# Ternary quantisation shared between VectorE and GpSimd, and three groupings of neighbouring work changed, in a post-norm layer of linear attention and a ternary FFN on eight cores

## The reference

```
# attention: 16 heads, 4 kv heads, D = 128
sq, sk = elu(q) + 1, elu(k) + 1
kv   = einsum('bhsd,bhse->bhde', sk, v)
qkv  = einsum('bhsd,bhde->bhse', sq, kv)
norm = einsum('bhsd,bhd->bhs', sq, sk.sum(axis=2))
attn = (qkv / (norm[..., None] + 1e-6)) @ Wo.T
# FFN: w1 is 8192 x 2048, w2 is 2048 x 8192
scale = mean(abs(w)); wq = sign(w) * (abs(w) >= 0.7 * scale)
h = gelu(x1 @ w1q.T + b1);  out = h @ w2q.T + b2
```

## Time and profile before

| | us |
|---|---|
| timed runs of the kernel | 5131.21 and 5246.88, median 5189.04 |
| the profiled execution, its time | 5129.48 |
| the profiled execution, its span on the slowest core (core 7) | 5127.9 |
| spans of the other cores | 5078.1 to 5113.5 |
| mean granted TensorE clock, cores 0 to 7 | 0.794 to 0.801 |

### The profile page before, as it was taken

How to read it: one execution, slowest core, us unless ns; L and a number is a source line. 1 busy time by engine, 2 the same in 40 slices (tenths; PEclk the granted TensorE clock), 3 DMA queues, 4 the chain that set the end, 5 groups by cost and what they waited for, 6 DMA issues and landing times.

```text
span 5127.9 us, 42520 instructions; the slowest of 8 cores (5078.1 to 5127.9 us)
## 1 busy us (share of the span) xinstructions
PE 2946.2 (57%) x11722; PEld 1193.0 (23%) x11722; DVE 1756.7 (34%) x3187; ACT 1045.0 (20%) x1473; POOL 493.9 (10%) x774
## 2 busy tenths in 40 slices
PE   2444445549765535555344342199960999609996
PEld 0111112113222112222111110033420444204442
DVE  0122223336433367777666664200123001230013
ACT  1566665553200100000000000011000110001100
POOL 1000000000011113333222221000000000000000
PEclk8677667769889768888666666599985999859998
DMA  9545554331233337777444442144521444214442
GB/s 168 160 148 152 154 156 108 107 103 29 56 103 95 105 86 185 184 184 191 133 135 142 147 130 77 64 136 152 150 88 58 137 151 155 88 61 138 150 156 107
DMA packets 215232, 644.62 MB, mean 126 GB/s; under 512 B 30674, under 2 KB 34770, under 8 KB 202708
## 3 DMA queue, kind: packets, MB, share of 16 engines
q1 hardware_dynamic: 161716, 486.66, 32.0%
q0 software_dynamic: 53280, 155.24, 10.8%
HBM read 578.87 MB, written 100.66 MB: 133 GB/s over the span
## 4 chain that ended last, share of the span: by engine, by line
PE 33%; DMA 26%; DVE 23%; ACT 8%; issue 8%; DVEq 1%; POOL 1%; ACTq 0%; SPq 0%; POOLq 0%
PE PB L825 16%; PE PB L770 11%; DMA arnE<-w 9%; DVE arnC L697 6%; DMA arnE<-xt 5%; DVE arnE L689 4%; DVE arnE L694 4%; PE PB L448 4%; DMA arnC<-w1q 3%; ACT arnE L263 3%; ACT arnE L268 3%; DMA out<-arnB 3%; DMA arnB<-y1s 2%; DMA w1q<-arnC 1%; PE PB L392 1%
## 5 line engine op out<-in xcount | busy, mean ns | idle before, releaser
L770 PE MATMUL PB<-arnB,arnC 128*128 128x512 bf16 x4096 | 984.7, 399 | 813.3 <-DMA arnC<-w1q 509.9
L825 PE MATMUL PB<-arnA,arnC 128*128 128x512 bf16 x4096 | 957.2, 399 | 432.4 <-DVE arnC L697 432.4
L770 PEld LDWEIGHTS PB<-arnB,arnC 128*128 128x128 bf16 x4096 | 403.2, 102 | 1399.0 <-issue 1008.6
L825 PEld LDWEIGHTS PB<-arnA,arnC 128*128 128x128 bf16 x4096 | 414.6, 102 | 974.6 <-issue 537.8
L838 DVE TENSOR_TENSOR arnB<-arnE,arnB 128x512 f32<-128x512 f32 x64 | 44.3, 692 | 1460.3 <-ACT arnE L834 1460.3
L779 ACT ACTIVATE arnA<-PB,b_sb 128x512 bf16<-128x512 f32 x256 | 176.4, 689 | 1076.8 <-PE PB L770 1076.8
L697 DVE SCALAR_TENSOR_TENSOR arnC<-arnE 128x512 bf16<-128x512 f32 x512 | 354.5, 692 | 95.6 <-DVE arnE L694 25.3
L564 PE MATMUL PB<-arnB,arnC 128*128 128x512 bf16 x1024 | 266.9, 422 | 149.0 <-DVE arnE L581 147.1
L263 ACT ACTIVATE arnE<-arnE 128x1024 f32<-128x1024 f32 x256 | 270.7, 1057 | 229.1 <-DMA arnE<-w 170.6
L834 ACT ACTIVATE arnE<-PB,b_sb 128x512 f32<-128x512 f32 x64 | 44.1, 689 | 1246.6 <-PE PB L825 1246.6
L275 DVE SCALAR_TENSOR_TENSOR acc<-acc_t,acc 128x1 f32<-128x1 f32 x256 | 40.8, 159 | 695.1 <-ACT arnE L268 691.4
(11 more groups left out here) (144 smaller groups left out, 1875.2 us busy)
## 6 DMA issues: line engine op xcount, KB each, us to landing
arnE<-w SPq DMA_DIRECT2D x256, 512.0 KB, 3.6
arnE<-w SPq DMA_DIRECT2D x512, 256.0 KB, 3.6
arnC<-w1q SPq DMA_DIRECT2D x192, 512.0 KB, 3.3
arnC<-w2q SPq DMA_DIRECT2D x96, 1024.0 KB, 5.9
w1q<-arnC POOLq DMA_DIRECT2D x256, 128.0 KB, 4.8
w2q<-arnC POOLq DMA_DIRECT2D x256, 128.0 KB, 2.7
arnE<-xt POOLq DMA_DIRECT2D x64, 256.0 KB, 3.9
y1s<-arnE POOLq DMA_DIRECT2D x64, 256.0 KB, 2.4
```

Of the source, the lines that this page charges most:

```text
L770: e.matmul(o, l, r, start=s, stop=z),
L825: e.matmul(o, l, r, start=s, stop=z),
```

## The change

Four things are done:

- In quant_piece the first compare (tb) and the difference (tqv, now tensor_tensor in place of scalar_tensor_tensor) go to GpSimd. The second compare (tg) stays on VectorE and waits for the load and for the tqv of the piece before. The lists vlast and clast, which held the tokens of the last pieces, go.
- emit_qkv and emit_qkv_B become one function again: the broadcast matmul is issued in the same step as the two read-out matmuls, and follows them in TensorE's queue. The read-out uses PB2 and PB3 alone. The waits for attnT_tok[15] at the start of the output projection go, since its banks PB5 and PB6 are used by nothing else by then.
- emit_ln1_dc is written into the loop over tiles: the first layer norm of tile t runs at the start of tile t, for all t, behind the whole last loop of the tile before.
- The bias of an output block is added on VectorE (tensor_scalar) and no longer on ScalarE (L834).

Core of the diff:

```diff
-    def emit_qkv_B():
-        ic, t, qp, j, tqkv, tr = qkv_pend.pop(0)
-        tbc = p.op("tensor", ... PB[4] <- ones_k1, row(2 + j) ...)
+    def emit_qkv(ic, t):
+        tqkv = p.op("tensor", ... PB[2] <- kv_l, sq_t ...
+                    waits=[sq_toks[ic][t], t_kv_ev, qkv_free], inc=sT)
+        tnrm = p.op("tensor", ... PB[3] <- ks_l, sq_t ...
+                    waits=[nrm_free], inc=sT)
+        tu = p.op("scalar", ... Ln ...);  tr = p.op("scalar", ... Exp ...)
+        tbc = p.op("tensor", lambda e, o=PB[4].ap(), l=ones_k1.ap(), r=r_r:
                    e.matmul(o, l, r, start=True, stop=True),
                    waits=[tr, rbc_free], inc=sT)
...
             sq_toks[ic][t] = m4_
-            emit_qkv_B()
             if ic >= 1:
                 emit_qkv(ic - 1, t)
...
-        tb = p.op("vector", lambda e, o=Esl(9), a=stage, b2=tneg:
+        tb = p.op("gpsimd", lambda e, o=Esl(9), a=stage, b2=tneg:
                   e.tensor_scalar(o, a, -C1H, b2, ALU.subtract, ALU.is_le),
-                  waits=[tok_d, thr_done, qres["b_free"],
-                         sqprev if first else None,
-                         abs_guard if first else None], inc=sV)
+                  waits=[tok_d, thr_done, qres["b_free"][0],
+                         abs_guard if first else None], inc=sP)
         tg = p.op("vector", lambda e, o=Esl(2), a=stage, b2=tpos:
                   e.tensor_scalar(o, a, C1H, b2, ALU.subtract, ALU.is_ge),
-                  inc=sV)
-        tqv = p.op("vector", lambda e, o=dst, a=Esl(2), b2=Esl(9):
-                   e.scalar_tensor_tensor(o, a, 1.0, b2, ALU.mult,
-                                          ALU.subtract),
-                   waits=[tb, tg] + list(dst_waits), inc=sV)
+                  waits=[tok_d, thr_done, qres["b_free"][1],
+                         sqprev if first else None], inc=sV)
+        tqv = p.op("gpsimd", lambda e, o=dst, a=Esl(2), b2=Esl(9):
+                   e.tensor_tensor(o, a, b2, ALU.subtract),
+                   waits=[tb, tg] + list(dst_waits), inc=sP)
         qres["stage_free"][sl] = tqv
-        qres["b_free"] = tqv
+        qres["b_free"][0] = tqv
+        qres["b_free"][1] = tqv
         tw = dma("gpsimd", dram_dst, dst, waits=[tqv])
...
     for t in range(NT):
-        for dc in (range(DC) if t == 0 else []):
-            emit_ln1_dc(t, dc)
+        for dc in range(DC):
+            (the body of emit_ln1_dc, with Esl(0) in place of Esl(1))
...
-            tv1 = p.op("scalar", lambda e, o=Esl(0), a=PB[2 + par].ap(),
+            tv1 = p.op("vector", lambda e, o=Esl(0), a=PB[2 + par].ap(),
                        b=b2_sb.ap()[:, dc:dc + 1]:
-                       e.activation(o, a, AF.Identity, bias=b),
-                       waits=[tmm, t_b2, ytmp_free], inc=sC)
+                       e.tensor_scalar(o, a, b, None, ALU.add),
+                       waits=[tmm, t_b2], inc=sV)
...
             x1_ready[dc] = None
-            if t + 1 < NT:
-                emit_ln1_dc(t + 1, dc)
```

More of the change, by code:

```diff
@@ L381, in build_nc @@
     thr_done = None
-    qkv_pend = []
-    def emit_qkv_B():
-        nonlocal rbc_free
-        if not qkv_pend:
-            return
-        ic, t, qp, j, tqkv, tr = qkv_pend.pop(0)
-        tbc = p.op("tensor", lambda e, o=PB[4].ap(), l=ones_k1.ap(),
-                   r=row(2 + j):
+    def emit_qkv(ic, t):
+        nonlocal qkv_free, nrm_free, rbc_free
+        kvh = ic // 4
+        kv_l = kvsb.ap()[:, kvh * 129: kvh * 129 + 128]
+        ks_l = kvsb.ap()[:, kvh * 129 + 128: kvh * 129 + 129]
+        sq_t = sq_tile(ic, t)
+        tqkv = p.op("tensor", lambda e, o=PB[2].ap(), l=kv_l, r=sq_t:
+                    e.matmul(o, l, r, start=True, stop=True),
+                    waits=[sq_toks[ic][t], t_kv_ev, qkv_free], inc=sT)
+        tnrm = p.op("tensor", lambda e, o=PB[3].ap()[0:1, :], l=ks_l, r=sq_t:
+                    e.matmul(o, l, r, start=True, stop=True),
+                    waits=[nrm_free], inc=sT)
+        qkv_last_mm[ic] = tnrm
+        j = (ic * NT + t) % 2
+        u_r, r_r = row(0 + j), row(2 + j)
+        tu = p.op("scalar", lambda e, o=u_r, a=PB[3].ap()[0:1, :],
+                  b=c_eps_at.ap():
+                  e.activation(o, a, AF.Ln, bias=b),
+                  waits=[tnrm, uro[j], st_["c_eps_at"],
+                         t_bkr if ic == 0 else None,
+                         t_bvr if ic == 0 else None], inc=sC)
+        nrm_free = tu
+        tr = p.op("scalar", lambda e, o=r_r, a=u_r, s2=c_none.ap():
+                  e.activation(o, a, AF.Exp, scale=s2),
+                  waits=[st_["c_none"]], inc=sC)
+        tbc = p.op("tensor", lambda e, o=PB[4].ap(), l=ones_k1.ap(), r=r_r:
                    e.matmul(o, l, r, start=True, stop=True),
@@ L400, in emit_qkv_B @@
                    o=Bbf[:, ic * 2048 + t * 512: ic * 2048 + (t + 1) * 512],
-                   a=PB[2 if qp == 0 else 5].ap(), b=Esl(0):
+                   a=PB[2].ap(), b=Esl(0):
                    e.tensor_mul(o, a, b), waits=[tqkv], inc=sV)
-        qkv_free[qp] = tdv
+        qkv_free = tdv
         if t == NT - 1:
             attnT_tok[ic] = tdv
[L407 to L436, removed]
     for ic in range(16):
@@ L664, in build_nc @@
     out_last = None
-    qres = {"rr": 0, "stage_free": [None] * 4, "b_free": None,
+    qres = {"rr": 0, "stage_free": [None] * 4, "b_free": [None, None],
             "wr_w1": [[None] * 4 for _ in range(64)],
-            "wr_w2": [[None] * 16 for _ in range(16)], "lastB": None,
-            "lastV": None, "usedC": False, "usedV": False}
+            "wr_w2": [[None] * 16 for _ in range(16)], "lastB": None}
     gwr_w1 = [[], []]
@@ L711, in w2q_slot @@
         return Cap[:, 4096 + (i % 3) * 4096: 4096 + ((i % 3) + 1) * 4096]
[L713 to L733, removed]
-    for t in range(NT):
-        for dc in (range(DC) if t == 0 else []):
-            emit_ln1_dc(t, dc)
+    for t in range(NT):
+        for dc in range(DC):
+            x1d = Bfap[:, dc * 512:(dc + 1) * 512]
+            x1b = Bbf[:, 16384 + dc * 512: 16384 + (dc + 1) * 512]
+            tld = dma("sync", x1d, y1s[t, dc],
+                      waits=[y1_wr[t][dc], x1_free[dc],
+                             wo_mm_done if t == 0 else None])
+            ta1 = p.op("vector", lambda e, o=Esl(0), a=x1d, b=Abc1(t):
+                       e.tensor_mul(o, a, b),
+                       waits=[tld, ab_done[t],
+                              y_free[0] if (t == 0 and dc == 0) else None,
+                              y_free[1] if (t == 0 and dc == 0) else None],
+                       inc=sV)
+            ta2 = p.op("vector", lambda e, o=x1d, a=Esl(0), b=Bbc1(t):
+                       e.tensor_add(o, a, b), inc=sV)
+            x1_ready[dc] = ta2
+            x1bf_ready[dc] = p.op("vector", lambda e, o=x1b, a=x1d:
+                                  e.tensor_copy(o, a), inc=sV)
         for fc in range(NFC):
@@ L751, in build_nc @@
                     wtoks.append(tw)
-                    if cf:
-                        clast = tqv
-                    else:
-                        vlast = tqv
-                w1q_tok[par] = [x for x in (vlast, clast) if x is not None]
+                w1q_tok[par] = tqv
                 gwr_w1[par] = wtoks
             else:
-                w1q_tok[par] = [dma(
+                w1q_tok[par] = dma(
                     "sync", buf, w1q[fc],
-                    waits=[w1q_free[par]] + qres["wr_w1"][fc] + gwr_w1[par])]
+                    waits=[w1q_free[par]] + qres["wr_w1"][fc] + gwr_w1[par])
                 gwr_w1[par] = []
```

42 lines of the change are left out of this document (12 added, 30 removed).

## The result

The changed kernel is slower: the ratio of its time to that of the kernel before is 1.2555, with a 95% interval of 1.2481 to 1.2629. Its fastest run took 6411 us, the fastest of before beside it 5111 us. The forecast was 5640 us with a range of 5380 to 6050; the sign was right, but the growth forecast, 510 us, is two fifths of the 1285 us that came, and the time lies outside the range. The profiled execution took 6414.5 us (span 6412.9, core 7, mean granted clock 0.738), against 5129.5 us (0.801). Times are compared between executions in which both dies ran at the same clock; durations of single instructions are in some cases (b_pool, c_fill, b_spw3 and the three kernels that take the compare apart) read from an execution in which one die was slower.

A forecast was written before the change was run, and what follows sets the result against it. No single engine bounds the kernel; each stage has its own limit, tile 0 running at the pace of VectorE's quantised pieces. 5129.5 + 620 (pieces) + 185 (read-out) - 295 (seams) = 5640 us, range 5380 to 6050.

The forecast's parts named there:

- pieces: 512 P - 1070: Tile 0's weight quantisation: growth from 512 pieces of period P on GpSimd; +620 us at P = 3.3.
- read-out in one step: Q stage: broadcast matmul waits for ScalarE's Exp, a group takes 8.26 instead of 5.24 us; +185 us.
- three seams: Between token tiles: separating the layer norm from the output loop saves 98.4 us at each seam; -295 us.
- bias on VectorE: Tile 0's w2 half: eviction takes about 0.75 us instead of 0.69 in the same chain; no growth counted.
- P = 1.34 + tb + tqv: Period of one quantised piece on GpSimd: DMA issue and its delay, two gaps, compare and difference in series.
- I take 3.3, a little under the middle: Chosen piece period in us, between 2.02 and 4.87, leaving 1.96 us for GpSimd's two passes, 1.7 times VectorE's.
- The upper end of P, 4.87: Longest piece period in us: each GpSimd pass as long as VectorE's 2048-column memset, 1.77 us.
- The prediction's estimate from that page: Piece period from the Trainium skill's GpSimd figures: P about 3.2, a sum some 50 us under the forecast.
- 13.5: Tile 0's w2 half: us per output block beyond its pieces, VectorE waiting for TensorE and eviction, then adding; unchanged.
- rival (c): Q stage: stalls lower TensorE's clock; if all 60 groups were slow, +270 us, 5910 us; chance 4%.
- (a): Tile 0's pieces: GpSimd as quick as VectorE, 4984 us at P = 2.02; chance 3% faster, 5% within 2%.
- (b): Tile 0's pieces: VectorE's and GpSimd's compares exclude each other, P = 4.0, 5998 us, up to 6443; chance 15%.

The follow-up runs named there:

- b_pool: The kernel before with only the first compare and the difference of each piece moved to GpSimd; ratio 1.2600.
- c_fill: The kernel before with the one-step attention read-out plus 13 unused matmuls per group while TensorE would wait; ratio 1.0304, fastest 5264 us.
- b_spw3: Compare and difference on GpSimd, each write DMA issued by SP four pieces later, otherwise the kernel before; fastest 6073 us.
- the three kernels that take the compare apart: Kernel before, compare and difference on GpSimd, the compare cut to one operation, made an addition, or given a constant operand; only durations read.
- g_bias: The kernel before with only the bias of an output block added by VectorE instead of ScalarE; ratio 1.0016.
- a_seams: The kernel before with only the next tile's first layer norm moved out of the last loop, behind it; ratio 0.9397, fastest 4799 us.
- b_spw: Compare and difference on GpSimd, each write DMA issued by SP ahead of the next piece's load, otherwise the kernel before; ratio 1.576.

## Why the prediction was wrong in size, by its own steps

| step | predicted us | in the changed kernel's trace us |
|---|---|---|
| pieces: 512 P - 1070 | +620 (P = 3.3) | +1289 (1239 + 1336 - 1286) |
| read-out in one step | +185 | +265 (830 - 565) |
| three seams | -295 | -296 |
| bias on VectorE | 0 | 0 (g_bias: ratio 1.0016) |
| sum on 5129.5 | 5640 | 6388, measured 6414.5 |

**The step that failed is a choice of value.** The sum's frame, P = 1.34 + tb + tqv, held: with 2.00 and 1.26 it gives 4.60, and 4.71 was measured; the rest is a DMA issue of 0.60 instead of 0.54, and gaps of 0.21 and 0.04 where I had 0.10 and 0.10. What failed was "I take 3.3, a little under the middle", with 1.96 us for both passes. They took 3.26, so the term for the pieces, +620 us, should have been +1289. The upper end of P, 4.87, held the truth, but I gave the upper part only 7% and cut the range there. That it held was in part luck: it let no pass take longer than 1.77 us, the compare took 2.00, and the sum stayed below it only because the difference took 1.26. The reason I gave, that these passes have 512 columns and the upper row 2048, was an argument about size, while the unknown was the engine. A common factor on VectorE's rows misled too: VectorE's tensor_scalar has 486 ns for two operations, less than its two-input pass of 692, and on GpSimd the order is reversed, 2001 against 1261. The factors are 4.1 and 1.8, and a common one of 1.7 fitted only the second. The Trainium skill (GPSIMD Engine Reference, section 3.1) has 769 ns for a one-input loop of 512 elements at its best; the measured 2001 ns, and 1567 with one operation, decide against it as a price for tensor_scalar. Its ratio of about two for two-input passes is near the 1.8 here, where VectorE's instruction was a scalar_tensor_tensor. The prediction's estimate from that page was, unrounded, P = 3.23 and 36 us under its sum and not some 50.

In the w1 half the stretch gives 4.84 us a piece (1239/256), and from the first L675 (2139.94) to the 256th (3357.71) it is 4.78. For the w2 half, TensorE's blocks:

```profile
3570.28 9.36 PE L784 MATMUL PB<-arnA,arnC 128*128 128x512 bf16 x32 [39.01 <-POOL arnC L675]
...
3656.28 4.00 PE L784 MATMUL PB<-arnA,arnC 128*128 128x512 bf16 x9 [39.01 <-POOL arnC L675]
```

86.0 us a block (3570.28 to 3656.28), where 16 x 4.71 + 13.5 would be 88.9. The next block's first compare runs on GpSimd from 3609.10, while VectorE still waits for TensorE, and only the difference waits for VectorE:

```profile
3621.44 1.26 POOL L675 TENSOR_TENSOR arnC<-arnE 128x512 bf16<-128x512 f32 x1 [10.34 <-DVE arnE L671]
```

So a block adds 10.6 us to its pieces (86.0 - 16 x 4.71) and not 13.5, and the formula was good to 3 us in 86.

**The read-out** was right in mechanism, and short by the clock. One line of ScalarE and three of TensorE in the changed kernel:

```profile
1443.05 0.72 ACT L404 ACTIVATE rows<-rows,c_none 1x512 f32<-1x512 f32 x1
...
1443.91 1.09 PE L407 MATMUL PB<-rows,ones_k 1*128 1x512 f32 x2 [2.91 <-ACT rows L404]
...
1444.94 5.31 PE L432 MATMUL PB<-arnA,arnC 128*128 128x512 bf16 x16
...
1453.69 1.09 PE L407 MATMUL PB<-rows,ones_k 1*128 1x512 f32 x2 [2.91 <-ACT rows L404]
```

L404 ends at 1443.77 and L407 starts 0.14 us later; it occupies 1.03 us. From the start of L432 to that of the next L407 it is 8.75 us, so the group takes 9.78 where I had 8.26. Of the 31 groups behind the last weights pass (1271.75 to 1582.91) 20 take 9.78 us, 9 about 11.1 and 2 take 8.09, as in c_fill; these two have the same pause of 2.9 us ahead of matmuls at the full clock. On average a group grew by 4.75 us there, and by 3.6 in the first eight blocks, where part of the wait hides beside the weights pass. The prediction's rival (c) had all groups wholly cold, +270 us on top of the sum, with a chance of 4%. What came is +80 on top, because most groups were partly cold (at the lower clock): 5.31 us lies between the 3.6 of warm and the 7.1 of cold matmuls. I had read that the w1 half of tile 0 with a mean clock of 0.86 has pauses of this kind, and charged 4 us for it and all else beyond the 181. This is the second term that was too small, by 80 us. c_fill settles that it is the pause.

**The seams** were right. The first output multiply and the last cast of the first seam, and TensorE there:

```profile
4754.00 0.69 DVE L857 TENSOR_TENSOR arnE<-arnB,arnE 128x512 f32<-128x512 f32 x1
...
4812.90 0.43 DVE L707 CAST arnB<-arnB 128x512 bf16<-128x512 f32 x1
```

```profile
4789.72 2.29 PE L736 MATMUL PB<-arnB,arnC 128*128 128x512 bf16 x5 [36.69 <-DMA arnC<-w1q]
```

4754.00 to 4813.33 is 59.3 us against 59.7 predicted and 158.1 before; the -296 in the table is three times this difference, and a_seams took 298 us off by itself. The DMA rate did not hold it.

**The rivals.** (a) is out by far. (b), that both engines shut each other out, is not what happened in the changed kernel: VectorE's compare fits, but for 0.06 us, in the 0.60 us before GpSimd's issue, and GpSimd's compare has 2000 to 2056 ns in all 512 cases. Its time of 5998 us came nearer than mine, by another cause, and that is luck. Where the two compares do start together (b_spw, b_spw3), GpSimd's grows by 0.27 us and VectorE's 0.49 stays; where GpSimd's starts first, VectorE's grows by 0.1 to 0.4 us. The Trainium skill (SBUF: State Buffer, section Who interferes with whom) has the second one blocked for the whole instruction of the first, if VectorE is in a 2-port mode (no run here shows in which mode it was); the runs agree that the second one waits, but VectorE's wait behind GpSimd's 2.00 us is 0.4 us at most.

## What to carry to other kernels

Before work is moved to an engine that does no arithmetic in the trace, its price per pass is the first thing to measure, and a range must keep the whole unknown: here the trim cut off what came, and even the untrimmed bound held for the sum of the two passes only, not for the compare. An engine that runs one piece's chain including its DMA issues pays for each link in series, so count the issue too (1.2 of 4.7 us), and do not put a waiting write in front of a load that ought to run ahead (b_spw: 1.58 against 1.26). Interleaving two loops is not an overlap when each step waits for a DMA round trip in order; separating them saved 6% here. A TensorE pause of 2.9 us in each group cost more than its length here (4.54 us in a group of 9.78), because the matmuls after it were slower. The largest gain on the kernel before that was found, 9%, needs none of the moves to another engine: it comes from the seams and from not letting VectorE's queue stand behind TensorE.

## What the runs showed of the hardware

- GpSimd on 128 x 512 float32: tensor_scalar with two operations 2.00 us, with one 1.57, with two operations whose operands are both constants 1.93; tensor_tensor with bf16 output 1.26. VectorE: 0.486 and 0.69.
- A GpSimd DMA issue starts 0.60 us after the instruction it waits for ends, both where VectorE's instruction released it and where GpSimd's own did, and takes 0.54 to 0.71 us.
- A tensor_scalar of each engine at the same time: started together, GpSimd's 2.00 becomes 2.27 and VectorE's stays at 0.49 (b_spw, b_spw3); VectorE's started 0.07 us behind takes 0.89, some 0.36 us behind 0.60, and GpSimd's stays at 2.00 (b_spw).
- 16 matmuls of 512 columns after a pause of 2.9 us mostly took 5.3 us instead of 3.6: the first nine or so are 0.43 us apart and the rest 0.21. In two groups of 31 they took 3.6 after the same pause. 13 unused matmuls in the pause made the kernel 105 us faster.
